# Second norm of the first two units from float32 products in PSUM, interleaved statistics and a new order of work, in a WKV and gated-FFN kernel

## The chip, the cores and the metric

The kernel runs on one core of a Trainium2 chip. Times are device microseconds of one launch, as a median over runs. The profile is one execution, recorded instruction by instruction; its times are counted from the start of its span. The engines are named PE (TensorE, with its weight loads as PEld), DVE (VectorE), ACT (ScalarE), POOL (GpSimd) and SP (SyncE, which issues the loads and stores here). Each works through its own list of instructions strictly in the written order and waits only on semaphores.

## The reference

Inputs are x and a context of 16 sequences x 128 steps x 256 channels, decays per channel, and a gated FFN of 704 inner channels with ternary weights and a scale per channel, all float32.

```python
def _layernorm(x, axis=-1, eps=1e-05):
    m = jnp.mean(x, axis=axis, keepdims=True)
    v = jnp.var(x, axis=axis, keepdims=True)
    return (x - m) / jnp.sqrt(v + eps)

def _wkv(time_decay, time_first, k, v):          # (16, 128, 256), step over 128
    w = -jnp.exp(time_decay)
    u = time_first
    def step(carry, kv_t):
        aa, bb, pp = carry
        kt, vt = kv_t
        ww = u + kt
        q = jnp.maximum(pp, ww)
        e1 = jnp.exp(pp - q)
        e2 = jnp.exp(ww - q)
        y_t = (e1 * aa + e2 * vt) / (e1 * bb + e2)
        ww2 = pp + w
        q2 = jnp.maximum(ww2, kt)
        e1b = jnp.exp(ww2 - q2)
        e2b = jnp.exp(kt - q2)
        return (e1b * aa + e2b * vt, e1b * bb + e2b, q2), y_t

def _L0_ffn_ref(x, gate_w, up_w, down_w, gate_s, up_s, down_s):
    xf = x.reshape(b * s, h)
    g = jnp.einsum('th,ih->ti', xf, gate_w) * gate_s      # 704 x 256
    u = jnp.einsum('th,ih->ti', xf, up_w) * up_s
    hdn = jax.nn.silu(g) * u
    return jnp.einsum('ti,hi->th', hdn, down_w) * down_s

x = x + _wkv(time_decay, time_first, _layernorm(x), ctx_2048)
x = x + _L0_ffn_ref(_layernorm(x), gate_w, up_w, down_w, gate_s, up_s, down_s)
```

## The kernel before

The 16 sequences are worked in 8 **units** of 2 sequences, and 2 units make a **group** of 512 tokens. The WKV part runs per unit, the FFN per group.

**First norm.** `xt` holds x with the time step on the partitions. `stats1(u)` on DVE (L533) and `aggr1(u)` (L539) give mean and variance of each sequence row, `rstd1` on ACT (L396, L398) the factor, `bias1` on POOL (L281, L283) the bias, and `expk(u)` on ACT (L405) writes `ek` = exp of the shifted norm. From unit 3 on, `rstd1` and `bias1` serve two units at once. The lists name them by the later unit.

**WKV.** `weigh` on POOL (L289) forms `ek` times v for units 0 to 3. `e_T` and `p_T` on PE (L679, L688) transpose both into the PSUM tiles `ps_a` and `ps_b`, so that channels lie on the partitions; for units 4 to 7 `mulp` on DVE (L548) forms the product in PSUM. DVE scans both over time (`scan_e` L558, `scan_p` L569) and adds the present step (`denom` L583, `numer` L593). ACT forms one over the denominator as exp of minus ln (`log_den` L414, `recip` L419). POOL multiplies (`divide` L305, into `yk`, two buffers) and adds y to the residual `xc` (`add_y` L311); `first` (L298) adds v of step 0, where y is v, for a whole group at once. `xc` is the channel-major copy of x, loaded in groups, and holds x + y after `add_y`.

**Second norm.** `x1_T` on PE (L698) transposes x + y back into a PSUM bank (`ps_x`; for unit 1 a bank of `ps_d`), `stats2` and `aggr2` on DVE (L600, L606) take the moments, the factor comes from ACT for units 0 and 1 (`rstd2a`, L424, L426) and from POOL for the others (`rstd2`, L321 to L327), `norm2` on ACT (L434) normalizes, `n_T` on PE (L706) transposes into channels again. `high_n` on ACT (L445) rounds to `xh`, and `low_n` on DVE (L616) writes the remainder `xl`, so that two fast products stand for one float32 product.

**FFN.** A group has 6 tiles of inner channels, 5 of 128 and one that packs the last 64 gate and 64 up channels. `gate(n)` and `up(n)` on PE (L728) are four matmuls each, into a ring of three PSUM slots `ps_f`. ACT applies silu (L465), DVE `gated` (L631) multiplies by the up half into `h`, ACT `high_h` (L476) and POOL `low_h` (L346) split h into `hh` and `hl`, and `down(n)` (L745) adds into `ps_d`. The ring sets waits: a slot filled by gate is free after silu, one filled by up after `gated`. The first three tiles of group 0 are made in two halves, `gatea`, `upa` for unit 0 and the rest for unit 1. `finish` on DVE (L643) adds the result to `xc`, and SP stores it. The last tiles of the last group make their two halves of `ps_d` separately (`downb`).

**Around it.** `whi(0..5)` on POOL (L334, L339) round the weights, piece by piece. `wcheck` on ACT (L456) sums the low halves of the weights' words; `count` and `publish` turn that into a flag on which PE branches to exact or rounded weights before the first product. `warm(k)` on PE (L756) are k float32 products of the identity that keep PE working while it has nothing to do. `tables` (L374) swaps ACT's function table between exp/ln and silu.

The order of all this is written by hand, one list of calls per engine, at the end of each engine's block; no scheduler changes it.

## Time and profile before

| | |
|---|---|
| median of 3 runs | 104.21 us (104.07 to 104.45) |
| span of the profiled execution | 102.7 us |
| busy: PE, DVE, ACT, POOL | 91.5, 80.0, 78.2, 66.8 us |
| first FFN product starts | 27.97 us |
| last product starts | 97.86 us |
| bytes read and written | 8.55 MB and 2.10 MB |

The profile lists no time for its execution besides the span, from the first instruction to the last; the median of the timed runs is 1.5 us above the span. A row of the timeline gives the start, the length in microseconds, engine, line, operation, the tile written and the tiles read, and in brackets how long the engine stood idle before and what released it. Two instructions that follow each other on an engine overlap by about a tenth of a microsecond, so the distance between two starts is what one costs its engine. A float32 product of the identity in `warm` is two records in the trace, a transposition one, and each product of the FFN one.

### The profile page before, as it was taken

The page shows a single profiled execution, that of the slowest core. Times are in us where ns is not written, and L with a number is a line of the kernel's source. Part 1 is how long each engine was busy: PE and PEld are TensorE (multiplying, and loading weights), DVE is VectorE, ACT ScalarE, POOL GpSimd, SP SyncE. Part 2 cuts the span into 40 slices and gives each one's busy share as a digit, 9 for nine tenths or more (in the row PEclk, how much of TensorE's full clock was granted, in tenths as well). Part 3 has the DMA queues.
Part 4 walks back from the last instruction along what each step waited for, and adds up shares of the span by engine and source line. Part 5 has one row for each costly group of instructions (what it writes and reads, how often), then busy time and mean ns, then how long its engine had stood idle before and what let it go on. Part 6 is the DMA issues. An engine that isn't in the chain of part 4 may idle for free.

```text
span 102.7 us, 1698 instructions
## 1 busy us (share of the span) xinstructions
PE 91.5 (89%) x504; PEld 75.1 (73%) x504; DVE 80.0 (78%) x169; ACT 78.2 (76%) x136; POOL 66.8 (65%) x96
## 2 busy tenths in 40 slices
PE   3958976998799999996999999999999999999930
PEld 3957965996596778875788887887888778888610
DVE  1789899969998999799999998999863806543450
ACT  4371999989997879999999999999959634655300
POOL 2016465998799999894399779827899701764500
PEclk9999999999999999999999999999999999999999
DMA  1999999999000000000005000000500000400005
GB/s 32 307 379 405 403 321 388 343 387 343 34 0 0 0 0 10 0 0 0 0 0 203 1 6 0 0 3 0 203 1 0 0 6 3 183 21 0 0 28 189
DMA packets 6475, 10.78 MB, mean 105 GB/s; under 512 B 576, under 2 KB 3648, under 8 KB 6336
## 3 DMA queue, kind: packets, MB, share of 16 engines
q1 hardware_dynamic: 6320, 10.62, 28.9%
q8 instruction: 6, 0.10, 0.4%
q10 hardware_dynamic: 144, 0.03, 0.2%
q14 instruction: 5, 0.04, 0.1%
HBM read 8.55 MB, written 2.10 MB: 104 GB/s over the span
## 4 chain that ended last, share of the span: by engine, by line
PE 27%; POOL 17%; ACT 15%; issue 14%; DMA 11%; DVE 6%; SPq 4%; POOLq 2%; DVEq 1%; ACTq 0%
PE ps_f L728 16%; DMA xc<-x_ch 11%; POOL hl L346 11%; PE ps_d L745 4%; ACT ek L405 4%; PE ps_f L756 3%; ACT L374 2%; POOL xc L311 2%; ACT nt L434 2%; SPq L228 2%; PE ps_x L698 2%; ACT xh L445 2%; DVE h L631 1%; POOL rs L323 1%; POOLq L59 1%
## 5 line engine op out<-in xcount | busy, mean ns | idle before, releaser
L728 PE MATMUL ps_f<-xh,wgu_r 128*128 128x512 f32 (+1 forms) x94 | 36.3, 391 | 0.6 <-DVE xl L616 0.4
L728 PE MATMUL ps_f<-xl,wgu_r 128*128 128x512 f32 (+1 forms) x94 | 35.1, 378 | 0.0
L346 POOL TENSOR_TENSOR hl<-h,hh 128x512 fp32r<-128x512 f32 x20 | 25.6, 1293 | 9.3 <-ACT hh L476 9.2
L631 DVE SCALAR_TENSOR_TENSOR h<-ps_f,vec,sil 128x512 f32<-128x512 f32 x20 | 14.9, 744 | 9.2 <-PE ps_f L728 6.2
L728 PEld LDWEIGHTS ps_f<-xh,wgu_r 128*128 128x128 f32 x94 | 17.7, 188 | 5.5 <-issue 1.4
L728 PEld LDWEIGHTS ps_f<-xl,wgu_r 128*128 128x128 f32 x94 | 17.7, 188 | 2.8
L756 PE MATMUL ps_f<-ident 128*128 128x128 f32 x110 | 15.5, 296 | 1.9 <-POOL ident L266 1.6
L465 ACT ACTIVATE sil<-ps_f,vec 128x512 f32<-128x512 f32 x20 | 13.7, 688 | 4.0 <-PE ps_f L728 3.8
L745 PE MATMUL ps_d<-hh,wd_r 128*128 128x512 f32 x40 | 16.3, 407 | 0.1
L756 PEld LDWEIGHTS ps_f<-ident 128*128 128x128 f32 x110 | 14.5, 211 | 2.1 <-POOL ident L266 1.6
L476 ACT ACTIVATE hh<-h 128x512 fp32r<-128x512 f32 x20 | 12.5, 629 | 4.6 <-DVE h L631 4.5
L745 PE MATMUL ps_d<-hl,wd_r 128*128 128x512 f32 x40 | 15.7, 393 | 0.0
L305 POOL TENSOR_TENSOR yk<-num,rden 128x508 f32<-128x508 f32 x8 | 10.2, 1281 | 2.1 <-DVE num L593 1.5
L374 ACT ACT_TABLE_LOAD x8 | 10.3, 1283 | 1.3 <-PEq L843 1.2
L405 ACT ACTIVATE ek<-xt,nb,rs 128x256 f32<-128x256 f32 x16 | 8.7, 595 | 2.9 <-POOL nb L283 2.8
L311 POOL TENSOR_TENSOR xc<-xc,yk 128x508 f32<-128x508 f32 x8 | 10.3, 1282 | 0.6
L558 DVE TENSOR_TENSOR_SCAN sbe<-decay,ps_a 128x512 f32<-128x512 f32 x8 | 9.6, 1204 | 0.4 <-PE ps_a L679 0.4
L569 DVE TENSOR_TENSOR_SCAN sbp<-decay,ps_b 128x512 f32<-128x512 f32 x8 | 9.6, 1205 | 0.0
L745 PEld LDWEIGHTS ps_d<-hh,wd_r 128*128 128x128 f32 x40 | 7.5, 188 | 2.2 <-POOL hl L346 0.7
L745 PEld LDWEIGHTS ps_d<-hl,wd_r 128*128 128x128 f32 x40 | 7.5, 189 | 1.4
L434 ACT ACTIVATE nt<-ps_x,nb,rs 128x256 f32<-128x256 f32 x14 | 7.1, 557 | 0.8 <-POOL nb L327 0.7
L679 PE MATMUL ps_a<-ident,ek 128*128 128x128 f32 x32 | 5.1, 281 | 2.4 <-ACT ek L405 2.2
(73 smaller groups left out, 133.8 us busy)
## 6 DMA issues: line engine op xcount, KB each, us to landing
xt<-x_tok SPq DMA_DIRECT2D x8, 256.0 KB, 7.3
...
wgu<-w_gu SPq DMA_DIRECT2D x1, 1408.0 KB, 8.6
...
wd<-w_d SPq DMA_DIRECT2D x1, 768.0 KB, 10.0
...
```

Source lines behind the costliest of these rows:

```text
L305: nc.gpsimd.tensor_tensor(yk[:, u % 2, :, 1:T], num[:, u % 2, :, 1:T], rden[:, u % 2, :, 1:T], ALU.mult).then_inc(s_y, 1)
L311: nc.gpsimd.tensor_tensor(later(xc, u), later(xc, u), yk[:, u % 2, :, 1:T].rearrange("p (c b) t -> p c b t", c=CC), ALU.add).then_inc(s_x1, 1)
L346: nc.gpsimd.tensor_tensor(hl[:, m, :], h[:, n % HS, :], hh[:, m, :].bitcast(F32), ALU.subtract).then_inc(s_hl, 1)
L374: nc.scalar.preload_act_table_set(name)
L405: last = nc.scalar.activation(ek[:, b, :], xt[:, b, :], ACT.Exp, scale=rs1[:, b:b + 1], bias=nb1[:, b:b + 1])
L465: nc.scalar.activation(sil[:, n % 2, :], f, ACT.Silu, scale=vec[:, V_GS + m:V_GS + m + 1]).then_inc(s_sil, 1)
L476: nc.scalar.activation(hh[:, m, :], h[:, n % HS, :], ACT.Copy).then_inc(s_hh, 1)
L558: nc.vector.tensor_tensor_scan(sbe[:, u % 2, :, :].rearrange("p q t -> p (q t)"), decay[:, :, :].rearrange("p q t -> p (q t)"), ps_a[:, :, ...
L631: nc.vector.scalar_tensor_tensor(h[:, n % HS, :] if m < FULL else up, up, vec[r, V_US + m:V_US + m + 1], sil[r, n % 2, :], ALU.mult, ALU.m ...
L728: last = nc.tensor.matmul(ps_f[:, i % RING, ts], w, a, start=c == 0 and x is xh, stop=c == CC - 1 and x is xl)
L745: last = nc.tensor.matmul(ps_d[:, c, :], wd_r[:, m, cs] if exact else wd[:, m, cs], a if exact else a.bitcast(F32), start=m == 0 and i == ...
L756: nc.tensor.matmul(ps_f[:, RING - 1, 0:P], ident[:, :], ident[:, :], start=True, stop=True)
```

## The change

- **x + y of units 0 and 1** is made in the PSUM bank itself. `x_T(u)` multiplies the identity with `xt` (128x512, float32) into the bank as soon as x is loaded, and `y_T(u)` adds y, transposed by four float32 products, when `divide` is done. `x1_T` stays for units 2 to 7. `add_y` of units 0 and 1 still writes `xc` for the residual, but nothing of the norm waits for it or for the load of `xc`. `lead(u)` puts v of step 0 into `yk`, and `first(0)` goes.
- **Three `yk` buffers** instead of two; `divide(u)` waits for `add_y(u-3)`, and `divide(3)` and `divide(4)` for `y_T(0)` and `y_T(1)` too.
- **Interleaved statistics**: one `bn_stats` per unit reads the two sequences element by element in turn (a hop of 256 words at each element, in `xt` and in PSUM), and its two half-results are the moments of the two sequences. `aggr1` and `aggr2` and their waits go; the 1/C is a scale at the users. In `rstd2` two one-column instructions without a wait between them take the place of `mr2` and `nb2`.
- **High parts first**: a product of the FFN does both `xh` matmuls before the `xl` ones, and the first of a group waits for `xl` only between them.
- **New order of work** on all four engines and of the loads on SP. Code for variants that were switched off (`settle`, `add_res`, `high_h` on POOL) goes.

```diff
-            load_x(0); load_x(1); load_x(2); load_x(3); load_v(0); load_v(1)
-            sp.dma_start(wgu[...], w_gu).then_inc(s_wgu, 16)
-            sp.dma_start(wd[...], w_d).then_inc(s_wd, 16)
-            load_res(0); load_v(2); load_x(4); load_x(5); load_v(3); load_res(1)
-            load_x(6); load_x(7); load_v(4); load_res(2); load_res(3)
+            load_x(0); load_x(1); load_x(2); load_x(3); load_v(0); load_v(1); load_wgu(); load_x(4); load_v(2)
+            load_wd(); load_x(5); load_res(0); load_x(6); load_res(1); load_x(7); load_res(2); load_v(3); load_res(3)
+            load_v(4)
...
+            def lead(u):
+                pool.wait_ge(s_vec, 16)
+                v0 = vec[:, V_V0:V_N].rearrange("p (c b) -> p c b", c=CC)[:, :, seqs(u)]
+                nc.gpsimd.tensor_copy(yk[:, u % YB, :, 0].rearrange("p (c b) -> p c b", c=CC), v0).then_inc(s_yv, 1)
...
             def divide(u):
                 pool.wait_ge(s_num, u + 1)
                 pool.wait_ge(s_rd, u + 1)
-                if u >= 2:
-                    pool.wait_ge(s_x1, u - 1)
+                if u >= YB:
+                    pool.wait_ge(s_x1, u - YB + 1)
+                    if u - YB < X1_PE:
+                        pool.wait_ge(s_x1T, u - YB + 1)
...
             def add_y(u):
                 pool.wait_ge(s_y, u + 1)
+                if u < X1_PE:
+                    pool.wait_ge(s_yv, u + 1)
+                    pool.wait_ge(s_xc[u // GU], 16)
+                    xs = xc[:, :, unit_cols(u)]
+                    nc.gpsimd.tensor_tensor(xs, xs, yk[:, u % YB, :, :].rearrange("p (c b) t -> p c (b t)", c=CC),
+                                            ALU.add).then_inc(s_x1, 1)
...
             def rstd2(u):
...
-                nc.gpsimd.tensor_tensor(mr2[:, seqs(u)], mv2[:, seqs(u), 0], rs2[:, seqs(u)], ALU.mult).then_inc(s_mr2, 1)
-                pool.wait_ge(s_mr2, u + 1)
-                nc.gpsimd.tensor_scalar(nb2[:, seqs(u)], mr2[:, seqs(u)], -1.0, 0.0, ALU.mult, ALU.add).then_inc(s_nb2, 1)
+                for b in range(u * UB, (u + 1) * UB):
+                    last = nc.gpsimd.tensor_scalar(nb2[:, b:b + 1], st2[:, b, 1:2], rs2[:, b:b + 1], -1.0, ALU.mult, ALU.mult)
+                last.then_inc(s_nb2, 1)
...
             def stats1(u):
                 dve.wait_ge(s_xt[u], 16)
-                for b in range(u * UB, (u + 1) * UB):
-                    last = nc.vector.bn_stats(st1[:, b, :], xt[:, b, :])
-                last.then_inc(s_st1, 1)
-
-            def aggr1(u):
-                dve.wait_ge(s_st1, u + 1)
-                for b in range(u * UB, (u + 1) * UB):
-                    last = nc.vector.bn_aggr(mv1[:, b, :], st1[:, b, :])
-                last.then_inc(s_mv1, 1)
+                nc.vector.bn_stats(st1[:, seqs(u), :].rearrange("p b k -> p (b k)"),
+                                   xt[:, seqs(u), :].rearrange("p b c -> p c b")).then_inc(s_st1, 1)
...
+            def x_T(u):
+                pe.wait_ge(s_xt[u], 16)
+                nc.tensor.matmul(x1_bank(u), ident[:, :], xt[:, seqs(u), :].rearrange("p b c -> p (b c)"), start=True, stop=False)
+
+            def y_T(u):
+                pe.wait_ge(s_y, u + 1)
+                pe.wait_ge(s_yv, u + 1)
+                for b in range(UB):
+                    for c in range(CC):
+                        last = nc.tensor.matmul(x1_bank(u)[:, b * C + c * P:b * C + (c + 1) * P], yk[:, u % YB, c * UB + b, :],
+                                                ident[:, :], start=False, stop=b == UB - 1 and c == CC - 1)
+                last.then_inc(s_x1T, 1)
...
-                if half == 0:
-                    pe.wait_ge(s_xl, 1)
-                elif m == 0 and part == 0:
-                    pe.wait_ge(s_xl, GU * (g + 1))
+                units = 1 if half == 0 else GU * (g + 1)
+                if half == 0 or m == 0:
+                    pe.wait_ge(s_xh, units)
...
-                for c in range(CC):
-                    for x in (xh, xl):
+                for x in (xh, xl):
+                    if x is xl and (half == 0 or m == 0):
+                        pe.wait_ge(s_xl, units)
+                    for c in range(CC):
...
-            warm(12); e_T(0); warm(5); p_T(0); warm(5); e_T(1); warm(8); p_T(1); e_T(2); warm(8); x1_T(0); warm(8)
-            warm(4); x1_T(1); count(); e_T(3); warm(2); p_T(2)
+            warm(10); x_T(0); x_T(1); warm(3); e_T(0); warm(7); p_T(0); e_T(1); warm(10); p_T(1); e_T(2); y_T(0)
+            warm(1); p_T(2); warm(8); y_T(1); e_T(3); count(); n_T(0)
```

Lines not shown: `stats2` changes as `stats1` does, `rstd1`, `rstd2a` and `rstd2` read `st1` and `st2` with a scale of 1/C. How the new lists stand is shown at three places.

POOL, from the first `divide` to the fourth. The rows name the operation and the tiles; `whi` is the CAST, `divide` writes `yk`, `add_y` writes `xc` from `yk`, `weigh` writes `vt`. Before:

```order
L305 TENSOR_TENSOR yk<-num,rden 128x4x127
L298 TENSOR_TENSOR xc<-xc,vec 128x2x4
L311 TENSOR_TENSOR xc<-xc,yk 128x2x2x127
L305 TENSOR_TENSOR yk<-num,rden 128x4x127
L311 TENSOR_TENSOR xc<-xc,yk 128x2x2x127
L334 CAST wgu_r<-wgu 128x2x384
L289 TENSOR_TENSOR vt<-vt,ek 128x512
L325 TENSOR_TENSOR mr2<-mv2,rs2 128x2
L327 TENSOR_SCALAR nb2<-mr2 128x2
```

Now:

```order
L322 CAST wgu_r<-wgu 128x2x384
L286 TENSOR_TENSOR yk<-num,rden 128x4x127
L262 TENSOR_TENSOR vt<-vt,ek 128x512
L327 CAST wd_r<-wd 128x768
L286 TENSOR_TENSOR yk<-num,rden 128x4x127
L314 TENSOR_SCALAR nb2<-st2,rs2 128x1 x2
L295 TENSOR_TENSOR xc<-xc,yk 128x2x256
L262 TENSOR_TENSOR vt<-vt,ek 128x512
```

The first `add_y` moved behind the second `divide` and behind the bias of unit 0's second norm, and a cast of each weight moved ahead of a `divide`.

ACT, its first rows after the constants: `lv1` and `rs1` are `rstd1`, `ek` is `expk`, `rden` from `den` is `log_den`. Before:

```order
L405 ACTIVATE ek<-xt,nb1,rs1 128x256 x2
L388 ACTIVATE elift<-lift 128x1
L396 ACTIVATE lv1<-mv1,epsc 128x2
L398 ACTIVATE rs1<-lv1 128x2
L405 ACTIVATE ek<-xt,nb1,rs1 128x256 x2
L396 ACTIVATE lv1<-mv1,epsc 128x4
L398 ACTIVATE rs1<-lv1 128x4
L414 ACTIVATE rden<-den,elift 128x4x127
L405 ACTIVATE ek<-xt,nb1,rs1 128x256 x2
```

Now:

```order
L379 ACTIVATE ek<-xt,nb1,rs1 128x256 x2
L370 ACTIVATE lv1<-st1,epsc 128x2
L372 ACTIVATE rs1<-lv1 128x2
L362 ACTIVATE elift<-lift 128x1
L370 ACTIVATE lv1<-st1,epsc 128x4
L372 ACTIVATE rs1<-lv1 128x4
L379 ACTIVATE ek<-xt,nb1,rs1 128x256 x4
L388 ACTIVATE rden<-den,elift 128x4x127
L379 ACTIVATE ek<-xt,nb1,rs1 128x256 x2
```

The factor of units 2 and 3 (the 128x4 rows) moved ahead of `expk(1)`, and `expk(2)` ahead of `log_den(0)`.

DVE, from about `stats2(3)` to past `denom(5)`: `h` and `ps_f` are `gated`, `den` is `denom`. Before:

```order
L539 BN_AGGR mv1<-st1 128x2 x2
L600 BN_STATS st2<-ps_x 128x6 x2
L539 BN_AGGR mv1<-st1 128x2 x2
L606 BN_AGGR mv2<-st2 128x2 x2
L631 SCALAR_TENSOR_TENSOR h<-ps_f,vec,sil 128x512
L631 SCALAR_TENSOR_TENSOR ps_f<-ps_f,vec,sil 64x512
L548 TENSOR_TENSOR ps_b<-ps_a,vc 128x512
L558 SCALAR_TENSOR_TENSOR sbe<-decay,ps_a 128x512
L569 SCALAR_TENSOR_TENSOR sbp<-decay,ps_b 128x512
L583 SCALAR_TENSOR_TENSOR den<-ps_a,fcol,sbe 128x2x127 x2
L616 TENSOR_TENSOR xl<-ps_x,xh 128x2x256
```

Now:

```order
L557 BN_STATS st2<-ps_x 128x6
L551 SCALAR_TENSOR_TENSOR num<-ps_b,fcol,sbp 128x2x127 x2
L506 TENSOR_TENSOR ps_b<-ps_a,vc 128x512
L516 SCALAR_TENSOR_TENSOR sbe<-decay,ps_a 128x512
L582 SCALAR_TENSOR_TENSOR h<-ps_f,vec,sil 128x512
L541 SCALAR_TENSOR_TENSOR den<-ps_a,fcol,sbe 128x2x127 x2
L582 SCALAR_TENSOR_TENSOR ps_f<-ps_f,vec,sil 64x512
L567 TENSOR_TENSOR xl<-ps_x,xh 128x2x256
L527 SCALAR_TENSOR_TENSOR sbp<-decay,ps_b 128x512
```

`denom(5)` moved ahead of `gated(5)` and of `scan_p(5)`, and the aggregations are gone.

## Rows read from the trace of the kernel before

**Rows 1.** The page: busy time, and the granted clock by slice.

```profile
PE 91.5 (89%) x504; PEld 75.1 (73%) x504; DVE 80.0 (78%) x169; ACT 78.2 (76%) x136; POOL 66.8 (65%) x96
...
PEclk9999999999999999999999999999999999999999
```

**Rows 2.** Stretches: from:to, length, busy PE PEld DVE ACT POOL, clock, DMA, GB/s.

```profile
18.05:27.97 9.92, 8.80 (x72) 7.51 (x73) 8.93 (x28) 9.49 (x22) 8.93 (x14) 1.00 0.80 284
...
31.70:46.40 14.70, 14.67 (x68) 10.92 (x68) 13.66 (x30) 12.89 (x24) 13.79 (x22) 1.00 0.01 2
46.40:98.30 51.90, 50.99 (x241) 40.95 (x240) 37.65 (x67) 40.12 (x62) 33.26 (x39) 1.00 0.09 32
```

**Rows 3.** The chain in order of time: start, length, what.

```profile
4.75 11.50 DMA xc<-x_ch
...
16.74 1.27 POOL xc L311
```

**Rows 4.** Timeline of ACT.

```profile
5.97 1.09 ACT L405 ACTIVATE ek<-xt,nb,rs 128x256 f32<-128x256 f32 x2 [0.65 <-POOL nb L283]
...
9.86 1.09 ACT L405 ACTIVATE ek<-xt,nb,rs 128x256 f32<-128x256 f32 x2 [2.16 <-POOL nb L283]
...
29.59 1.28 ACT L374 ACT_TABLE_LOAD   x1
30.88 1.27 ACT L465 ACTIVATE sil<-ps_f,vec 128x512 f32<-128x512 f32 x2
```

**Rows 5.** Timeline of DVE.

```profile
3.72 0.75 DVE L533 BATCH_NORM_STATS2 st<-xt 128x6 f32<-128x256 f32 x2
...
46.28 0.85 DVE L583 SCALAR_TENSOR_TENSOR den<-ps_a,fcol,sbe 128x254 f32<-128x254 f32 x2
```

**Rows 6.** DVE, groups of instructions by form: busy, mean ns, idle before.

```profile
L533 DVE BATCH_NORM_STATS2 st<-xt 128x6 f32<-128x256 f32 x16 | 5.9, 414 | 0.5 <-DMA xt<-x_tok 0.5
...
L606 DVE BATCH_NORM_AGGREGATE mv<-st 128x2 f32<-128x6 f32 x16 | 1.9, 160 | 0.1
...
L569 DVE TENSOR_TENSOR_SCAN sbp<-decay,ps_b 128x512 f32<-128x512 f32 x8 | 9.6, 1205 | 0.0
```

**Rows 7.** POOL, groups by form.

```profile
L325 POOL TENSOR_TENSOR mr<-mv,rs 128x2 f32<-128x2 f32 x8 | 1.6, 195 | 0.6
...
L298 POOL TENSOR_TENSOR xc<-xc,vec 128x8 f32<-128x8 f32 x4 | 0.8, 212 | 1.2 <-DMA xc<-x_ch 1.2
```

**Rows 8.** Timeline of POOL.

```profile
8.06 1.27 POOL L289 TENSOR_TENSOR vt<-vt,ek 128x512 f32<-128x512 f32 x1 [2.19 <-DMA vt<-v_tok]
...
13.88 1.26 POOL L305 TENSOR_TENSOR yk<-num,rden 128x508 f32<-128x508 f32 x1 [0.59 <-ACT rden L419]
```

**Rows 9.** Issues of loads on SP: KB each, us from issue to landing.

```profile
wgu<-w_gu SPq DMA_DIRECT2D x1, 1408.0 KB, 8.6
wd<-w_d SPq DMA_DIRECT2D x1, 768.0 KB, 10.0
```

**Rows 10.** Timeline of PE.

```profile
31.71 0.47 PE L728 MATMUL ps_f<-xh,wgu_r 128*128 128x512 f32 x1 [0.20 <-ACT sil L465]
...
46.03 0.40 PE L745 MATMUL ps_d<-hl,wd_r 128*128 128x512 f32 x1
47.28 0.63 PE L679 MATMUL ps_a<-ident,ek 128*128 128x128 f32 x4 [0.85 <-ACT ek L405]
...
96.39 0.39 PE L745 MATMUL ps_d<-hl,wd_r 128*128 128x512 f32 x1
96.83 0.50 PE L745 MATMUL ps_d<-hh,wd_r 128*128 128x512 f32 x1
...
97.86 0.63 PE L745 MATMUL ps_d<-hx,wd_r 128*128 128x512 f32 x2
```

**Rows 11.** `warm` alone: stretch, length, busy PE (records), PEld, clock, DMA, GB/s.

```profile
2.50:3.50 1.00, 1.00 (x7) 1.00 (x7) 1.00 1.06 371
...
4.50:5.00 0.50, 0.50 (x6) 0.50 (x5) 1.00 0.99 262
```

202 lines of the change are left out of this document (76 added, 126 removed).

## The prediction

> **What bounds the kernel now.** I read the busy shares first [rows 1]: PE works 91.5 of 102.7 us, so the question is when it can start and where it stalls. The stretches [rows 2] answer: from 31.7 on PE is full (14.67 of 14.70, then 50.99 of 51.90). Its busy share of 8.80 in 9.92 us before the products is no demand; most of that is `warm`. So the span is a lead-in of 31.7 us, set by others, then PE's list at 0.23 us per 512-column product, then a tail. Three things can move the end: when PE's full stretch starts, the stalls in it, and the work in it.
>
> The lead-in ends with silu(0): the first product into a reused ring slot starts at 31.71 and was released by silu [rows 10], and silu(0) starts at 30.88, behind the table load at 29.59 [rows 4]. Back from there ACT is full (9.49 of 9.92 us [rows 2]) but for waits early on: 0.65 us for the bias of unit 0 and 2.16 us for that of unit 1 [rows 4]. The chain [rows 3] names another cause, the load of `xc`: 11.50 us until 16.25, then `add_y(0)` at 16.74. Both stand on the way, but ACT, which has no gap to give, decides what moving the load is worth.
>
> In the full stretch I look for starts further apart than 0.23 us. The big one is 46.03 to 47.28 [rows 10], so 1.02 us lost, before `e_T(6)`. The row blames `ek`, but `e_T(6)` waits for `denom(5)` too, and that runs from 46.28 to 47.13 [rows 5]. At the end 96.39 to 96.83 holds 0.21 us of waiting for `low_h(22)`; the last pair of products starts at 97.86 [rows 10].
>
> **Part 1, x + y in PSUM, and the loads.** Today `divide(0)` starts at 13.88 and is done by 15.14 [rows 8], and `add_y(0)` starts only at 16.74 and takes 1.27 [rows 3], so x + y is ready at 18.01. `y_T(0)` needs `divide(0)` alone. `whi(0)` now stands ahead of it and waits for `wgu`, which lands 8.6 us after its issue at 3.76, so 12.4 [rows 9]; with 0.8 us for the cast POOL is free at 13.2, and `divide(0)` starts near 13.6. The statistics of unit 0 can be 3 us earlier. What does it cost? `x_T` is 512 float32 columns, eight records of 128 columns by `warm`'s size, 0.9 us each, in a place where `warm` shrank from 12 to 10; `y_T` takes about 0.9 us against 0.5 for a transposition. PE has room for both. Putting `wd` behind `xt` of unit 4 and v of units 2 and 3 moves it from 14.3 [rows 9] to about 17 by its place in the queue; `whi(4)` and with it `divide(1)` wait for it, to 17.8. But `recip(1)` on ACT comes at 18.0 by the sum below, so that is covered; if the load came 1 us later, `divide(1)` and the second norm of unit 1 would be that much later. `xc` of group 0 now lands near 19 and its first reader comes at 19.5.
>
> **Part 2, the start of silu(0).** ACT's list up to silu(0) holds the same instructions before and after, so its end moves by its start and its gaps. Start: without `aggr1(0)` and with one instruction of an estimated 0.67 us in place of two of 0.75 together [rows 5], the variance is there at 4.4 instead of 4.75: 0.35 us. (0.67: a 256-element read takes 414 ns, and 1 us per 960 elements of it is length, so 512 take 414 + 267 = 0.68 [rows 6]; the lower bound is 0.6, the upper is the scan of 512 at 1.2.) Gaps: today 0.65 + 2.16 = 2.8 us [rows 4]. The 2.16 is there because POOL does `weigh(0)` first, which waits for v until 8.06 [rows 8]; now `bias1(1)` is ahead of it. In its place stands `rstd1(3)`, moved ahead of `expk(1)`: it needs `stats1(3)`, which DVE finishes near 8.2, while ACT arrives at 7.15. That is 1.05 us idle, and 0.2 us more for the bias of units 2 and 3, which waits behind `weigh(0)`. With 0.6 for unit 0's bias: 1.85 left of 2.8, gain 0.95. Together **1.3 us**: silu(0) at 29.6.
>
> Do the others keep up? DVE's list to `gated(0)`: 9 scans at 1.1, 8 `denom` and `numer` at 0.8, 5 statistics at 0.65 and 1.3 of the rest, 21 us from 8.1, and 0.6 for waits: 29.7, against sil(0) at 30.2. Close: 0.5 us of cover. POOL has the bias of unit 0's second norm at 19.5 and ACT asks at 19.7; of unit 1's at 23.2 and 23.3. So three engines meet within half a microsecond at several places. That is why I don't take the full 1.6 that one pass through the lists without friction gives.
>
> **Part 3, the stall at 46 us.** Between `gated(0)` and the end of `denom(5)` DVE loses `gated(5)`, `scan_p(5)`, `scan_e(4)` and four pairs of aggregations (0.8 + 1.1 + 1.1 + 0.7) and gains `mulp(4)` and `stats1(6)` (0.7 + 0.6): 2.4 us less, on top of the earlier start. `denom(5)` is done near 43, before PE asks for it. What is late next? `down(4)` wants `low_h(4)`, which now stands behind `divide(4)`, `first(3)` and `add_y(4)` on POOL: three operations, 2.8 us; I find it at 46.2 where PE asks at 45.9. Gain of the 1.02: 0.7 to 1.0, and smaller stalls near 34 and 38 us of today that go or stay would balance the new one: **1.0**.
>
> **Part 4, the end.** `down(18)` moved behind `gate(23)`, so 0.92 us more work covers the wait for `low_h(22)`: **0.2 us**. The tail after the last product is unchanged. PE's own work in the full stretch is unchanged: same products, same transpositions. High parts first lets the first product of a group start before `xl`; that is hidden where PE is behind anyway, so nothing for it.
>
> **The sum.** 1.3 + 1.0 + 0.2 = 2.5 us off a span of 102.7: 100.2. The median lies 1.5 above the span, so 104.2 - 2.5 = **101.7 us**.
>
> **A rule against it.** The interleaved read hops 256 words at each element. No row of DVE shows such a read. The nearest is POOL's: `first` reads 8 elements with hops of 128 words in 212 ns where 2 elements take 195 [rows 7], 2.8 ns per element and no more than its plain rate (1.26 us for 508 elements [rows 8]); so I take no penalty. The Trainium skill, "Vector Engine (DVE) Microarchitecture Reference", section on the SBUF access granule, says that a port is at full rate only if its elements come in adjacent pairs, and gives 1.73 against 1.05 ns per column when one source hops at each element; but it also reports one stream that alternates between two regions at the full rate. By 1.73 a statistic would cost about 1.0 us, an estimate from that page, which lies inside the first rival's bounds; no run here shows it yet.
>
> **Rivals.**
> - *The hop costs some.* Halfway between 0.67 and the scan's 1.2 [rows 6], 0.95 each. Of the nine statistics before `gated(0)` two hide behind the loads of x; seven cost 7 x 0.3 = 2.1 us, less 0.5 of cover. That is 1.6, more than the 1.3 of Part 2, so the start is 0.3 later than today; Parts 3 and 4 remain: 0.3 - 1.0 - 0.2 = -0.9, 103.3 us.
> - *The hop costs double* (slower). At 1.2, the length of a scan: 7 x 0.53 = 3.7, less 0.5 of cover, less the 1.3: the start is 1.9 later than today. Four more statistics before `denom(5)` take 2.1 of its 2.4, so the stall goes only in part: +1.9 - 0.4 - 0.2 = +1.3, 105.5 us. It turns against the change once a statistic costs over 1.1 us.
> - *Head of line.* With the new order some wait of 1 to 1.5 us forms where the three engines meet (`divide(1)` behind `whi(4)`, `rstd1(3)` ahead of `expk(1)`, `low_h(4)`): 102.9 us. For it speaks how full all lists are [rows 2]; against it that no single link above lacks more than 0.4 us.
> - *PE's clock.* Between `n_T(0)` and silu(0) PE now has about 5 us of work in 9, with no `warm`. `warm` shows both levels: 7 records in 1 us early (half speed, 1.2 GHz), 12 per us from 4.5 on, 2.4 GHz [rows 11], while the granted clock reads full throughout [rows 1]. If PE fell back to the lower level at 28, its first products would take 0.46 instead of 0.23; 5 us of work would be 10, some of it behind silu: +2.5, so 104.2, no change. The Trainium skill, "TensorE: Matmul & The Clock Gate", says that an idle stretch brings the lower clock back and that transpositions may not count as work; the longest gap I count is 1.3 us.
> - *Not what it says.* The start is ACT's, so x + y earlier could be worth nothing by itself. I have priced that: Part 1 has no term of its own. What it does is let the second norm run without holding ACT up.
>
> **How the numbers follow.** A measurement of this kernel can tell about 0.5% from no change, 103.7 to 104.7. Forecast 50%. Hop costs some 22%, three quarters of it faster, the rest within 0.5%. Head of line 12%, mostly faster. Clock 7%, no change. Double hop 9%, slower. Faster 0.77, same 0.13, slower 0.10. Below, the range starts at 100.6: the friction-free pass gives 1.6 + 1.3 + 0.2 = 3.1 us, and 0.5 for what I miss. Above, it takes in the two middle rivals with 0.4 for their bounds, 103.7; what lies outside is the double hop, most of the clock case and little below.
>
> **What would show it.** Right: silu(0) starts at 29.3 to 30.0; a statistic takes 0.6 to 0.7 us; `e_T(6)` starts without a gap; the last product starts near 95.4; distances of 0.23 between products throughout. Wrong: a statistic at 0.95 or more and `gated(0)` later than 31; a gap over 0.5 us before 50 us at another place; products 0.46 apart at 28 to 32; a wait of ACT for `rstd1(3)` longer than 1.5 us.

## The result, and the profile after

The changed kernel takes **106.11 us** (median of four executions, 105.57 to 106.58) where the kernel before takes 104.14 on the same chip (103.82 to 104.45): ratio 1.0189, interval 1.0153 to 1.0225. The change makes the kernel slower by 1.9%. The forecast was 101.7, faster by 2.4%.

The kernel before has, on some chips, a second group of executions at 105.2 to 106.4 us, and every ratio below is taken without them and on one chip, so a ratio tells more than two medians side by side.

The page of the profiled execution (105.73 us, span 103.8), lines as in [rows 1]: the span, the busy time and the granted clock by slice of 2.6 us.

```profile
span 103.8 us, 1619 instructions
...
PE 91.5 (88%) x484; PEld 75.0 (72%) x484; DVE 77.0 (74%) x121; ACT 77.4 (75%) x136; POOL 68.0 (65%) x97
...
PEclk9999999999958999999999999999999999999975
```

PE is busy for the same 91.5 us, but two of its slices near 30 us were granted a lower clock (5 and 8 tenths), and the last two as well. Before, the row was full.

The lead-in did what the prediction said, in this execution. ACT, timeline, as in [rows 4]:

```profile
5.79 1.09 ACT L379 ACTIVATE ek<-xt,nb,rs 128x256 f32<-128x256 f32 x2 [0.65 <-POOL nb L256]
...
8.51 1.08 ACT L379 ACTIVATE ek<-xt,nb,rs 128x256 f32<-128x256 f32 x2
...
29.19 0.69 ACT L439 ACTIVATE sil<-ps_f,vec 128x512 f32<-128x512 f32 x1
```

`expk(1)` starts at 8.51 in place of 9.86 and silu(0) at 29.19 in place of 30.88: 1.69 us won against this execution of before. It is a late one: in three more traces with its lists silu(0) starts at 30.45, 30.43 and 29.86 (`before_again`, and the two below with only a wait added at the end). But PE, timeline, as in [rows 10], doesn't get it:

```profile
20.63 0.66 PE L668 MATMUL ps_x<-ident,nt 128*128 128x128 f32 x4
23.31 0.48 PE L691 MATMUL ps_f<-xh,wgu_r 128*128 128x256 f32 x2 [2.02 <-issue]
...
26.06 0.48 PE L691 MATMUL ps_f<-xh,wgu_r 128*128 128x256 f32 x2
28.34 0.66 PE L691 MATMUL ps_f<-xl,wgu_r 128*128 128x256 f32 x2 [1.80 <-DVE xl L567]
...
30.08 0.63 PE L691 MATMUL ps_f<-xl,wgu_r 128*128 128x256 f32 x2
30.51 0.63 PE L691 MATMUL ps_f<-xh,wgu_r 128*128 128x256 f32 x2
30.93 0.63 PE L691 MATMUL ps_f<-xl,wgu_r 128*128 128x256 f32 x2
31.36 0.63 PE L691 MATMUL ps_f<-xh,wgu_r 128*128 128x512 f32 x1
```

There are two idle stretches, 2.02 us (`n_T(0)` is done, the branch on the flag is not taken yet; DVE writes the flag at 21.92) and 1.80 us (the low part of gate(0) waits for `low_n(1)`). After the second, pairs of 256-column products start 0.42 to 0.43 us apart, where before single ones start 0.117 apart. The first 512-column product starts at 31.36, against 31.71 before: 0.35 of the 1.69 us are left. The stretches, columns as in [rows 2]:

```profile
22.00:24.00 2.00, 0.69 (x6) 0.72 (x7) 2.00 (x6) 1.91 (x5) 1.34 (x4) 1.00 1.06 389
24.00:26.00 2.00, 2.00 (x20) 2.00 (x19) 1.90 (x4) 2.00 (x5) 2.00 (x3) 1.00 0.78 292
26.00:28.00 2.00, 0.54 (x5) 0.33 (x3) 1.90 (x4) 1.98 (x5) 2.00 (x3) 1.00 0.03 13
28.00:30.00 2.00, 1.66 (x8) 1.66 (x9) 1.52 (x3) 1.86 (x2) 2.00 (x3) 0.63 0.01 4
30.00:32.00 2.00, 2.00 (x10) 1.90 (x9) 1.74 (x3) 0.40 (x1) 1.69 (x5) 0.52 0.00 0
```

The granted clock is 0.63 and then 0.52, so most of 28 to 32 us runs at the lower of the two levels, 1.2 GHz.

At the far end, the last pair of products starts at 97.55, 0.31 us before its old place [rows 10], yet the span is 1.1 us longer. SP's waits (us in total, times, longest):

```profile
SPq L58 <- DMA out_ch<-xc: 3.6, 1, 3.6
```

The last store is waited for 3.6 us; before, 2.2. So this pair of executions wins 0.3 us up to the last product and loses 1.4 behind it.

A second look at each kernel shows what one profile hides.

> The kernel before, unchanged, for a second trace beside the changed kernel on one chip. If the 0.229 us between products and the 2.2 us wait for the last store are the kernel's own, they come again here; if they vary from one execution to the next, a part of what the change's trace shows (0.2335 us and 3.6 us) is no effect of the change.

Before, again: 104.19 us, span 102.3, wait for the last store 2.2.

> The changed kernel, unchanged. Theory (clock): the granted clock falls to half between 28 and 32 us again, products there stand 0.46 us apart for 256 columns twice, the mean clock is 0.97. Rival (chance of one execution): a trace with the clock full throughout and a span near 100.5 us. The distance of products later, 0.2335 or 0.229 us, and the wait for the last store, 3.6 or 2.2 us, are open.

Changed, again: 107.07 us, span 105.2, wait for the last store 3.8, and silu(0) starts at 31.70, 2.5 us later than in the first profile. Its lead-in had already lost 1.3 us at 9 us. The last product starts at 98.73, where `before_again` has 97.47, so this pair loses 1.3 us ahead of it: the 0.3 us won above are no gain to count on. PE, timeline, of the first profile and, in the second fence, of this one:

```profile
1.58 3.93 PE L719 MATMUL ps_f<-ident 128*128 128x128 f32 x20 [1.58 <-POOL ident L247]
5.35 1.02 PE L653 MATMUL ps_x<-xt,ident 128*128 128x512 f32 x2
6.21 1.02 PE L653 MATMUL ps_d<-xt,ident 128*128 128x512 f32 x2
...
7.74 0.60 PE L628 MATMUL ps_a<-ident,ek 128*128 128x128 f32 x4
```

```profile
1.58 4.64 PE L719 MATMUL ps_f<-ident 128*128 128x128 f32 x20 [1.58 <-POOL ident L247]
6.01 1.71 PE L653 MATMUL ps_x<-xt,ident 128*128 128x512 f32 x2
7.55 1.02 PE L653 MATMUL ps_d<-xt,ident 128*128 128x512 f32 x2
...
9.08 0.60 PE L628 MATMUL ps_a<-ident,ek 128*128 128x128 f32 x4
```

`warm(10)` takes 3.93 us in the one and 4.64 in the other, and `x_T(0)` 1.02 and 1.71: PE comes to its higher clock at a different time in each execution. `expk(0)` is done at 6.9 both times, and `e_T(0)` waits behind that queue until 7.74 or 9.08. In before nothing but `warm(12)` stands ahead of `e_T(0)`; it started at 7.12 and 7.11 in the two profiles.

So three suspects stand: the clock near 28 us, `e_T(0)` behind the two `x_T`, and the last store.

### The profile page after: what moved, and what is told of

It reads as the page before. It is cut to its first block, busy times and chain, and to the rows that moved or that the text cites. A ratio compares the mean times of both kernels' runs of the same rounds, so it can differ in the third digit from the quotient of the medians.

```text
span 103.8 us, 1619 instructions
## 1 busy us (share of the span) xinstructions
PE 91.5 (88%) x484; PEld 75.0 (72%) x484; DVE 77.0 (74%) x121; ACT 77.4 (75%) x136; POOL 68.0 (65%) x97
## 4 chain that ended last, share of the span: by engine, by line
PE 64%; DVE 20%; issue 5%; ACT 4%; DVEq 1%; POOL 1%; POOLq 0%; ACTq 0%
PE ps_f L691 35%; PE ps_d L708 17%; DVE sbe L516 5%; DVE sbp L527 5%; PE ps_f L719 4%; DVE den L541 3%; PE ps_x L647 3%; DVE num L551 2%; ACT L348 2%; DVE xl L567 2%; PE ps_a L628 2%; PE ps_x L668 2%; DVEq L58 1%; PE ps_x L653 1%; PE ps_d L653 1%
## 5 line engine op out<-in xcount | busy, mean ns | idle before, releaser
L691 PE MATMUL ps_f<-xh,wgu_r 128*128 128x512 f32 (+1 forms) x94 | 30.3, 404 | 2.2 <-issue 2.0
L691 PE MATMUL ps_f<-xl,wgu_r 128*128 128x512 f32 (+1 forms) x94 | 29.0, 391 | 1.8 <-DVE xl L567 1.8
L691 PEld LDWEIGHTS ps_f<-xl,wgu_r 128*128 128x128 f32 x94 | 17.8, 196 | 5.9 <-DVE xl L567 2.3
L691 PEld LDWEIGHTS ps_f<-xh,wgu_r 128*128 128x128 f32 x94 | 17.0, 198 | 6.0 <-issue 2.2
L439 ACT ACTIVATE sil<-ps_f,vec 128x512 f32<-128x512 f32 x20 | 13.6, 686 | 5.5 <-PE ps_f L691 5.3
L719 PE MATMUL ps_f<-ident 128*128 128x128 f32 x78 | 11.2, 303 | 1.6 <-POOL ident L247 1.6
L719 PEld LDWEIGHTS ps_f<-ident 128*128 128x128 f32 x78 | 10.7, 217 | 2.1 <-POOL ident L247 1.6
L299 POOL TENSOR_TENSOR xc<-xc,yk 128x508 f32<-128x508 f32 x6 | 7.7, 1282 | 0.2
L551 DVE SCALAR_TENSOR_TENSOR num<-ps_b,fcol,sbp 128x254 f32<-128x254 f32 x16 | 6.9, 473 | 0.4
```

Source lines behind the costliest of these rows:

```text
L439: nc.scalar.activation(sil[:, n % 2, :], f, ACT.Silu, scale=vec[:, V_GS + m:V_GS + m + 1]).then_inc(s_sil, 1)
L551: last = nc.vector.scalar_tensor_tensor(num[:, u % 2, q, 1:T], ps_b[:, q, 1:T], fcol[:, c:c + 1], sbp[:, u % 2, q, 0:T - 1], ALU.mult, ALU ...
L691: last = nc.tensor.matmul(ps_f[:, i % RING, ts], w, a, start=c == 0 and x is xh, stop=c == CC - 1 and x is xl)
L719: nc.tensor.matmul(ps_f[:, RING - 1, 0:P], ident[:, :], ident[:, :], start=True, stop=True)
```

## The clock, filled and unfilled

**e1_fill**: the changed kernel with filling products in the two idle stretches.

```diff
-            ... e_T(3); count(); n_T(0)
+            ... e_T(3); count(); n_T(0); warm(4)
...
-                ... gatea(1); e_T(4); gate(0); x1_T(2); ...
+                ... gatea(1); e_T(4); warm_d(8); gate(0); x1_T(2); ...
```

> The changed kernel with 4 more identity products behind n_T(0) and 8 ahead of the second half of gate(0), in PSUM columns that nothing else uses then; nothing else differs. Theory (the clock fell because PE had too little to do between 20.6 and 28.3 us): the granted clock stays full, the product after silu(0) starts near 30.0 instead of 31.36, and the time falls by 1.3 to 1.8 us, to 104.3 to 104.8. Rival (the clock falls for another reason, or the loss lies in the waits of the lists): the clock falls as before or the time stays within 0.4 us of the changed kernel.

105.05 us (103.86 to 105.84, ten executions), ratio 1.0045 (0.9985 to 1.0105). The granted clock stays full, and the kernel is 1.1 us faster than without the filling by the medians, 1.5 by the ratios, though it does more work; the intervals of the two ratios don't touch. The median is a little above the 104.3 to 104.8 that I expected, and the last product starts at 97.24, hardly earlier: in this execution `e_T(0)` came late (8.99) and silu(0) with it (30.45). `warm_d(8)` ran from 27.39 to 29.1 and did not stand in the way. The low part of gate(0) had to wait for `low_n(1)` in any case, as DVE and PE show:

```profile
28.86 0.68 DVE L567 TENSOR_TENSOR xl<-ps_d,xh 128x512 fp32r<-128x512 f32 x1
...
29.59 0.51 PE L691 MATMUL ps_f<-xl,wgu_r 128*128 128x256 f32 x2
```

Two expectations below say that the eight ran 0.8 us past `low_n(1)`; these rows show that they did not.

**e2_nowarm**: the kernel before without its own filling around `x1_T(1)`, `p_T(2)` and `n_T`, 17 identity products.

```diff
-                warm(2); n_T(0); warm(1); n_T(1); ...
+                n_T(0); n_T(1); ...
...
-            ... warm(8); x1_T(0); warm(8)
-            warm(4); x1_T(1); count(); e_T(3); warm(2); p_T(2)
+            ... warm(8); x1_T(0)
+            x1_T(1); count(); e_T(3); p_T(2)
```

> The kernel before, without the 28 identity products between p_T(1) ... x1_T(1) and the first FFN product except 8: removed are the 12 around x1_T(1), the 2 ahead of p_T(2) and the 3 around n_T(0). Theory: PE has little to do from 18.5 to 28 us, the granted clock falls near 28 and the time rises by 1.5 to 2.5 us though the identity products computed nothing. Rival: the clock holds, and the time is the same within 0.3 us, because the removed work was idle time anyway.

104.75 us (104.21 to 105.83), ratio 1.0067 (1.0028 to 1.0105). The clock fell as expected. Stretches of this kernel, columns as above:

```profile
20.00:22.00 2.00, 1.30 (x12) 1.03 (x13) 1.69 (x12) 1.97 (x6) 2.00 (x3) 0.70 1.10 365
22.00:24.00 2.00, 1.65 (x9) 1.25 (x8) 1.20 (x2) 1.91 (x7) 1.66 (x8) 0.50 1.04 384
24.00:26.00 2.00, 1.92 (x8) 1.32 (x8) 2.00 (x5) 2.00 (x5) 1.76 (x3) 0.50 0.76 281
```

But the time rose by 0.7 us where 1.5 to 2.5 was expected: here the lower clock ran while ACT was full (1.97, 1.91 and 2.00 of 2 us), and it was over (1.00 at 28 to 30) before the products came. The profiled execution lost nothing by it: its last product starts at 97.75, and the two profiles of before have 97.86 and 97.47. Where the 0.7 us lie is not shown. What a fallen clock costs depends on whose turn it is.

## The last store: first the wrong cause

SP issues its loads in another order in the changed kernel. I suspected that this moves the last store to a worse place in some queue. **f1_after_loads** is the changed kernel with the old order of loads, **f2_before_loads** the kernel before with the new one, **f3_fill_loads** is e1_fill with the old order; the edit is in each the list of `load_...` calls, the other kernel's taken over whole.

> The changed kernel with the order of the loads on SP of before, nothing else. In the profiled executions of the changed kernel the last store's landing is waited for 3.6 to 3.8 us on SP, in those of before 2.2. Theory A, the order in which SP issues its loads decides on which of the transfer engines or at which place of a ring the last store falls, and one piece of it comes late: with the old order the last wait is 2.2 to 2.5 us and the kernel gains about 1.3 us, 104.8. Theory B, the lateness comes of something else that the change does at the end (groups finished at other times, the clock of the chip's other parts): the wait stays at 3.4 to 3.8 us and the time at 106. In both the clock of TensorE still falls near 28 to 32 us.

> The kernel before with the order of the loads on SP of the changed kernel, nothing else. Theory A (load order makes the last store late): the last wait on SP grows from 2.2 to some 3.6 us and the time from 104.1 to 105.5. Theory B: the wait stays at 2.2 and the time within 0.4 us of before, unless x_ch for group 0 or the weights come later than they are wanted; in that case the first FFN product moves and the chain up to silu(0) shows it, not the tail.

> The changed kernel with the filling products (4 behind n_T(0), 8 ahead of gate(0)) and the order of the loads of before. Theory A: both losses gone, clock 1.0 and last wait 2.2 to 2.5 us: 105.05 - 1.3 = 103.7, under the kernel before by some 0.5 us. Theory B: as the kernel with the filling products alone, 105.0, with a last wait of 3.4 us. Neither theory expects 101.7, since the filling products did not bring the last product forward by more than 0.2 us against before.

Theory A falls three times. f1: 106.36 us (ratio 1.0254, 1.0195 to 1.0313), the last store still waited for 3.4. f2: 108.84 (1.043, 1.0358 to 1.0502), the wait unchanged at 2.2. f3: 105.87 (1.0165, 1.0124 to 1.0206), the wait 3.3. What f2 does show is worth having: before needs `xc` early, and with the new order it landed at 18.4 in place of 16.25, where the clock fell at 19 as well (granted 5, 5 and 7 tenths in three slices from 18.8 us on), and silu(0) started at 35.68. Taking x + y from PSUM is what lets `xc` come late. So the old order does not help the changed kernel, and the lists' order and the loads' belong together.

One thing came out against the expectation of f1. In its profiled execution the granted clock stayed full, without any filling, though PE stood idle for 1.73, 0.91 and 1.81 us between 16 and 30 us and worked 0.18 of the 2 us from 28 on. An idle stretch of this length doesn't bring the lower clock back every time.

## The last store: a transfer of code

What else moves data at the end? The queues and kinds of transfer in narrow stretches of the changed kernel's trace show it. Below: 100.6 to 100.7, then 101.3 to 102.0, then 102.0 to 103.1 (packets that start there; q1 carries the store; share is of 16 engines).

```profile
DMA packets 22, 0.06 MB, mean 573 GB/s; under 512 B 1, under 2 KB 1, under 8 KB 21
...
q1 hardware_dynamic: 21, 0.04, 115.4%
q8 instruction: 1, 0.02, 86.3%
...
DMA packets 0, 0.00 MB, mean 0 GB/s; under 512 B 0, under 2 KB 0, under 8 KB 0
...
DMA packets 9, 0.02 MB, mean 15 GB/s; under 512 B 1, under 2 KB 1, under 8 KB 9
...
q1 hardware_dynamic: 9, 0.02, 6.0%
```

Amid the last store, at 100.64, one packet of 16 KB on the queue for instructions starts and takes 1.38 us (86.3% of 16 engines over 0.1 us is 1.38). By 101.3 the rest of the store is through; then for 0.7 us nothing starts; then, from 102.0 on, as the code transfer ends, nine last packets of the store follow one behind the other, until 103.0. A store of 256 KB is 144 packets here, and nine are a sixteenth of them, so I take them for the share of the one engine that carried the code; the trace doesn't name the engine of a packet. Before, the stretches 101.5 to 101.75 and 101.75 to 102.7 read:

```profile
q1 hardware_dynamic: 3, 0.00, 4.5%
...
q8 instruction: 1, 0.02, 6.6%
```

The same transfer starts at 101.84, when the store's last packet has ended at 101.72, 0.1 us earlier.

Whose code? Such a transfer stands 3.7 to 3.9 us earlier too: at 97.92 before, 0.06 us behind the start of the last pair of products, and at 96.95 in the changed kernel, 0.6 us ahead of it. Before, PE waits for `low_h(22)` and `hx` in its last products; in the changed kernel it waits for nothing there (Part 4 of the prediction). So I suspected that its sequencer has run ahead and reaches the jump out of the branch sooner, and that both transfers come sooner by that. It can be tested by holding the sequencer.

**g1_end_wait**: the changed kernel with one wait behind the last product.

```diff
                 down(23); downb(23)
+                pe.wait_ge(s_tail[1], 1)
```

> The changed kernel, with one wait added behind TensorE's last product: it waits for that product's own end before it leaves the branch. In every trace so far two transfers of 16 KB on the queue for instructions follow each other by some 3.8 us at the end. In before the first starts 0.1 us after the last product's start (97.92) and the second (101.84) when the last store has landed (101.72). In the changed kernel, where TensorE waits for nothing in its last products, the first starts 0.6 us ahead of the last product (96.95) and the second (100.64, for 1.38 us) amid the last store, whose last packets come 1.7 us after the others. Theory C: TensorE's sequencer fetches code when it has issued its last product and jumps, and the second transfer holds one of the 16 DMA engines that the store needs; with the wait both transfers come 0.8 us later, the second begins as the store ends, the last wait on SP is 2.2 to 2.5 us in place of 3.6, and the time is some 1.2 us lower, 104.9. Rival D: these transfers belong to another engine or the late packets to something else, and the wait on SP stays at 3.4 to 3.8 us with the time unchanged at 106.1 or 0.1 above.

The two transfers moved with the wait: none from 96.5 to 100.6, then one at 100.73 and one at 103.83. So they are PE's code. The gain is half of what was expected or less: 105.45 us (105.05 to 105.95), ratio 1.0158 (1.0114 to 1.0202). That is 0.7 us by the medians and 0.3 by the ratios, and the interval overlaps that of the changed kernel (1.0153 to 1.0225), so this run alone shows no gain. In this execution the last product started at 98.57, so the first transfer came 2.2 us behind it and fell into the start of the store; the wait went from 3.6 to 2.9. In the six other traces with the wait it comes 1.6 to 1.7 us behind the last product.

**g2_eT_first** puts `e_T(0)` ahead of the two `x_T`; **g3_all** has that, the wait at the end, and filling of 4 and 4.

```diff
-            warm(10); x_T(0); x_T(1); warm(3); e_T(0); warm(7); p_T(0); ...
+            warm(12); e_T(0); x_T(0); x_T(1); warm(3); p_T(0); ...
```

> The changed kernel with e_T(0) ahead of x_T(0) and x_T(1) (12 identity products, e_T(0), the two x_T, 3 identity products, p_T(0)). In two executions of before TensorE's clock first rises at 4.81 and at 7.25 us and scan_e(0) starts at 7.97 and 7.91; in executions of the changed kernel it rises at 4.62, 5.22, 6.49, 7.20 and 7.38 and scan_e(0) starts at 8.45, 8.73, 9.34, 9.70 and 9.79, since the two x_T stand ahead of e_T(0). Theory E (head of line): scan_e(0) comes at 7.9 to 8.0 whenever the clock rises, silu(0) comes at 28.6 or so, and the median falls by 0.5 to 1.2 us, to some 105.2, the clock's fall near 28 us and the late store remaining. Rival F: the lead-in is bound by DVE and ACT behind scan_e(0), or the x_T now delay p_T(0) by as much; silu(0) stays at 29.2 to 31.7 and the time at 106.

> The changed kernel with all three: the wait at the end, e_T(0) ahead of the two x_T, and filling products (4 behind n_T(0), where TensorE waits for the branch, and 4 ahead of gate(0); the 8 of the run before ran past low_n(1) by 0.8 us). If the three losses are independent and complete: 106.1 less 1.2 (store) less 0.9 (e_T(0)) less 1.3 (clock) = 102.7, below before by 1.3% or so. If the clock is the only real one: 104.8. If the lead won in the lead-in is given back in later stages (e_T(6), waits for silu) as the filling products alone suggested (last product only 0.2 us earlier than in before): 103.5 to 104.

g2: 106.06 us, ratio 1.0239 (1.012 to 1.0359). scan_e(0) came at 8.42 and not at 7.9 to 8.0, the clock fell at 23 us, and silu(0) came at 30.32 and not at 28.6. Alone, this edit shows no gain.

g3: **103.04 us** (102.86 to 103.36, seven executions), ratio **0.9937** (0.9909 to 0.9965). Its page, and its wait for the last store:

```profile
span 101.2 us, 1631 instructions
...
PEclk9999999999999999999999999999999999999999
...
SPq L58 <- DMA out_ch<-xc: 2.0, 1, 2.0
```

Its code transfers start at 97.50 and 100.58, and the store's last packet ends at 100.18.

## One edit at a time out of the best version

By the medians the single edits on the changed kernel gave 1.1, 0.7 and nothing, the three together 3.1; by the ratios, which leave out the difference between chips, 1.5, 0.3 and -0.5, together 2.6. Alone, only the filling is clear of noise. The order in which losses are removed matters, so each was also put back alone.

> The best version (all three edits, 103.0 us) without the wait at the end. If the code transfers of TensorE amid the last store are a loss of their own (theory C), the second of them starts some 4.8 us after the last product but one again, falls into the last store, the wait on SP is 3.4 to 4.2 us in place of 2.0 and the time 104.2 to 104.6. If the last store came in time in the best version for another reason, 103.0.

> The best version without e_T(0) ahead of the two x_T (they stand ahead of it again). If head of line is a loss of its own (theory E) that depends on when TensorE's clock first rises, scan_e(0) comes at 8.4 to 9.8 in place of 7.94, silu(0) as much later, and the time is 103.5 to 104.8 with a wide spread, where the best version's seven times lie within 0.5 us. If not, 103.0.

> The best version without the filling products behind n_T(0) and ahead of gate(0). If the clock is a loss of its own, it falls to half between 23 and 28 us for 3.4 us, and the time is 104.0 to 104.6. The two single edits (end wait 105.4, e_T(0) first 106.1) were worth 0.7 and nothing, the three together 3.1: a reason could be that a late fall of the clock eats what e_T(0) gives; then this one is near 105.4.

| kernel | us | ratio to before (interval) | against 103.0 |
|---|---|---|---|
| g3, all three | 103.04 | 0.9937 (0.9909 to 0.9965) | |
| h1, no wait at the end | 104.31 | 1.0055 (1.0022 to 1.0088) | +1.3 |
| h2, x_T ahead of e_T(0) | 104.01 | 1.0032 (0.9989 to 1.0075) | +1.0 |
| h3, no filling | 105.04 | 1.0108 (1.0071 to 1.0146) | +2.0 |

Each interval lies above that of g3, and by the ratios the three prices are 1.2, 1.0 and 1.8 us.

h1: the second transfer starts at 99.07 for 1.67 us, again amid the store. Stretches 99.8 to 100.7 and 100.7 to 101.8 of its trace, and SP's wait:

```profile
DMA packets 0, 0.00 MB, mean 0 GB/s; under 512 B 0, under 2 KB 0, under 8 KB 0
...
q1 hardware_dynamic: 9, 0.02, 6.0%
...
SPq L58 <- DMA out_ch<-xc: 3.9, 1, 3.9
```

The same picture as in the changed kernel: nothing starts until the code transfer is over, then nine packets. With the wait 2.0, without it 3.9, and 1.3 us of time.

h2: `e_T(0)` at 8.33 in place of 6.84, scan_e(0) at 9.04 in place of 7.94, silu(0) at 29.80 in place of 28.99. Its five times spread over 1.4 us (103.09 to 104.47), those of the best version over 0.5 (0.8 in its second series, below).

h3: in this execution the clock fell twice. Stretches:

```profile
24.00:26.00 2.00, 2.00 (x12) 2.00 (x11) 1.46 (x3) 1.23 (x3) 2.00 (x3) 0.50 0.54 199
...
28.00:30.00 2.00, 0.19 (x3) 0.04 (x1) 1.90 (x5) 1.98 (x3) 1.24 (x2) 1.00 0.00 0
30.00:32.00 2.00, 2.00 (x10) 2.00 (x11) 1.60 (x2) 1.00 (x2) 1.38 (x3) 0.56 0.01 4
```

First after the idle stretch at the branch; the slow work from 23 to 27 pushed `low_n(1)` back, PE idled for 1.8 us again, and the clock fell a second time under the first products. That fits g2, where `e_T(0)` first gained nothing without the filling. The profiled execution is one of its two slowest (106.4); its median is 105.04.

## On one chip, and what before's second group is

> The best version (wait at the end, e_T(0) ahead of the two x_T, 4 + 4 filling products) once more, on another chip if it is one. Expected 103.0 with all its times within 0.6 us, 0.6% under before's lower group of times and 2% under its upper one; last product 95.9 to 96.1.

> The changed kernel itself beside them on the same chip. Expected 105.6 to 107.4 as before, 2.6 to 3.2 us over the best version; the first rise of TensorE's clock (4.6 to 7.4 us) sets scan_e(0), and the clock falls for 3.4 us between 24 and 32.

> The changed kernel with the filling products alone (4 + 4, where the first run with them had 4 + 8). If the clock alone is worth what its removal from the best version cost (2.0 us), 104.1 to 104.4; the eight ahead of gate(0) ran 0.8 us past the landing of low_n(1) and the kernel took 105.05. The late store (3.4 to 4.2 us) and scan_e(0) at 8.4 to 9.8 stay.

> The kernel before with the wait at the end alone. Before has two groups of times, some 103.6 to 104.2 and some 105.4 to 106.4 us, on this and on other chips. In its profiled executions of the first group the second code transfer starts 0.1 to 0.3 us after the last store has landed. If the second group is the executions in which it starts a little earlier and falls into the store, the wait at the end takes it away: all times at 103.6 to 104.2. If the second group has another cause, it stays, at a share of about one half.

> The kernel before with the wait at the end, again. Its six times lay at 103.98 to 104.68 where three or four of eleven times of before beside them lay at 105.2 to 105.8. If the second group is the store held up by code transfers, no time is over 104.9 again; if it was chance, two or three of the six are near 105.5.

i1, the best version again: 103.13 us (103.01 to 103.80, eleven), ratio 0.9928 (0.9899 to 0.9958), last product at 95.77. i2, the changed kernel beside it: 106.49 (105.30 to 106.89, six), ratio 1.0169 (1.0102 to 1.0237). Its execution at 105.30 has a mean granted clock of 0.99, the other five, at 106.10 and above, 0.966 to 0.972: the clock doesn't fall every time, and the one without the fall is the shortest. i4, filling 4 and 4 alone: 105.13 (104.16 to 105.97, twelve), ratio 1.0066 (1.0032 to 1.0100), expected 104.1 to 104.4; in its profile `x_T` held `e_T(0)` back (scan_e(0) at 9.45) and the last store was waited for 4.2 us. On this chip the filling is worth 1.4 us from i2 to i4 (1.1 by the ratios), and the other two edits 2.0 from i4 to i1, which h1 and h2 priced at 1.3 and 1.0. From the other side (h3) the filling is worth 2.0. And 4 products ahead of gate(0) did no better than 8 (ratio 1.0066 against 1.0045 in e1_fill).

The end of i4 shows something that the account of the last store lacks. Stretches 100.77 to 101.06, 101.06 to 101.10 and 102.05 to 103.10 of its trace:

```profile
DMA packets 0, 0.00 MB, mean 0 GB/s; under 512 B 0, under 2 KB 0, under 8 KB 0
...
q8 instruction: 1, 0.02, 159.2%
...
q1 hardware_dynamic: 9, 0.02, 6.3%
```

The other fifteen shares of the store are through by 100.77. Then nothing starts for 0.3 us, the code transfer starts at 101.07 (for 1.02 us), and the nine packets follow. All packets of the store before it had started by 100.05, so the late share stood still for 1.0 us ahead of the code packet; in i2 it was 0.9 and in g2 1.1. What holds it in that time is not shown: that the two meet in time is not the whole mechanism. The transfer even starts 3.98 us behind the last product here, exactly as in before, where the store went through. What the traces do show is a tally. The nine packets were late in all nine traces of the changed lists without the wait, in none of the four of before's lists, and with the wait in none of the seven but g1, where the store's last packet came 0.6 us behind the other shares.

h4, the kernel before with the wait at the end: six times from 103.98 to 104.68, ratio 1.0061 (1.0038 to 1.0084), beside four of eleven executions of before at 105.2 or more. i3, the same again: eleven times from 104.15 to 105.07 (a twelfth, at 316.84, is left out), two of them over the 104.9 that I had set as the limit; ratio 1.0032 (0.9999 to 1.0065). There only two of 28 executions of before were above 105.3, so it could not decide. That before's times above 105.2 are stores held up in the same way stays a guess: none of them was profiled. In before itself the wait costs 0.3 to 0.6 us.

## Why the prediction was wrong, point by point

- **Part 1** (x + y in PSUM, and the loads): right in what it gave. `divide(0)` starts at 13.73 (said: near 13.6), the second `divide` at 17.30 (said: wait until 17.8). Wrong in "PE has room for both". The room was not ahead of `e_T(0)`: the two `x_T` and the products around them stand there, `e_T(0)` starts 0.9 to 2.2 us after its input, and by how much is set by the time at which the clock first rises. So this is a first step that failed: a price of 1.0 us (h2) that the sum put at nothing. The rival "head of line" had the mechanism and 1 to 1.5 us, but looked for it on ACT and POOL.
- **Part 2** (silu(0) at 29.6): right where the clock rises early, 29.19 and 29.48 in two profiles (29.19 is 1.7 below this execution of before and 1.3 below `before_again`); 31.70 in the third. Right on the statistic: 0.68 to 0.72 us against 0.67, from `xt` in SBUF and from PSUM alike, so the rival "the hop costs" is out. By the estimate from the Trainium skill ("Vector Engine (DVE) Microarchitecture Reference", on the SBUF access granule) it would have been 1.0; what agrees is the other case that page reports, one stream that alternates between two regions at full rate.
- The earlier silu(0) is worth what was said if the clock holds: in the best version silu(0) comes at 28.99 and the first 512-column product at 29.93, 1.8 us before its place in the first profile of before and 1.35 before that in the second. With the fallen clock it comes at 31.36. **The largest step that failed is PE's clock**, which the sum put at nothing and the rival at 7%, for the reason that the longest gap I counted was 1.3 us. The trace has 2.02 and 1.80. The first comes from the branch: `n_T(0)` moved from behind it to ahead of it, and with it went the `warm` that stood around `n_T(0)` there; before, the same spot shows 0.31 us of idle time. I priced the change's transpositions and products on PE and never laid out when PE would stand still. The rival's size was near: 1.1 to 2.0 us where I had said 2.5, and its place was right in the first profile (products slow at 28 to 32). The Trainium skill, "TensorE: Matmul & The Clock Gate", Part 1 (the clock gate), says that an idle stretch brings the lower clock back; this trace agrees: PE worked 0.69 of the 2 us from 22 on and 0.54 of the 2 us from 26 on, and then the clock fell. In f1 it did not fall after stretches of 1.73, 0.91 and 1.81 us, so by these traces it happens often and not always.
- **Part 3** (the stall before `e_T(6)`, 1.0): right on the stall, wrong on its worth. The row of after has no gap, in PE's timeline:

```profile
44.80 0.39 PE L708 MATMUL ps_d<-hl,wd_r 128*128 128x512 f32 x1
45.03 0.60 PE L628 MATMUL ps_a<-ident,ek 128*128 128x128 f32 x4
```

  But at equal content PE is ahead of before by 0.46 us at `n_T(3)`, ahead of the stall, and by 0.93 at `n_T(4)`, behind it: of the 1.02 us only 0.5 arrive. At `n_T(6)` it is 0.85, and 0.5 goes again before `n_T(7)`, the larger part in one wait of 0.35 us near 70 us for sil(13), which stands behind a table load. That one the prediction missed.
- **Part 4** (the end, 0.2): the wait for `low_h(22)` is gone. "The tail after the last product is unchanged" is a further step that failed, by 1.4 us (3.6 for 2.2). By the traces it comes of that very gain: a PE that waits for nothing at its end leaves its branch earlier, and its first code transfer starts 0.6 us ahead of the last product in place of 0.06 behind it. Price 1.3 us (h1).
- **The sum.** What is left without the three losses is read best against `before_again`, whose 104.19 us is close to before's median. PE's first 512-column product and its last one, in `before_again` and then in the best version:

```profile
31.28 0.47 PE L728 MATMUL ps_f<-xh,wgu_r 128*128 128x512 f32 x1
...
97.47 0.62 PE L745 MATMUL ps_d<-hx,wd_r 128*128 128x512 f32 x2
```

```profile
29.93 0.62 PE L691 MATMUL ps_f<-xh,wgu_r 128*128 128x512 f32 x2
...
95.87 0.63 PE L708 MATMUL ps_d<-hx,wd_r 128*128 128x512 f32 x2
```

  The start is 1.35 us earlier: the 1.3 of Part 2. From there to the last product PE needs 65.94 us (65.84 in i1) for 66.19 (66.15 in the first profile of before): 0.3 us won, where **Parts 3 and 4 had 1.2. This term was too large by 0.9.** The new waits are 0.25 us at 36.6 and 0.35 at 68.5, and PE's own work did not stay the same: two products that follow each other start 0.233 us apart on average where before they start 0.230 apart, which makes 0.6 us over 220 pairs. It is so in every trace of the changed lists, for `down` too, whose code did not change; the cause is open. Behind the last product the best version needs 5.3 us of span for 4.8. SP's last two issues take 1.65 us there in place of 0.99, in traces where the first code transfer, moved by the wait, falls into them. Together 1.1 us where the prediction had 2.5, hence 103.0 and not 101.7. That the last product, at 95.8 to 95.9, comes near the 95.4 of the prediction is in part luck: the 102.7 us of the first profile are a late execution. (Time less span is 1.9 us in `before_again` as in the best version; the 1.5 came of setting one execution's span against the median of others.) The miss of 4.4 us is 3.1 for the three losses together (2.6 by the ratios; singly 1.1 to 2.0, 1.0 and 1.3) and 1.3 for the rest: about 0.9 in the full stretch and 0.5 behind it.
